# Decays of four turned states made ahead in three buffers, a row's first scan before the last product, and three smaller moves in a state-space kernel

## The reference

```
def _selective_scan(x, x_proj_w, dt_proj_w, dt_proj_b, A_log, Dp):
    A = -jnp.exp(A_log)
    dbc = jnp.einsum('bld,nd->bln', x, x_proj_w)
    delta, Bm, Cm = jnp.split(dbc, [DT_RANK, DT_RANK + D_STATE], axis=-1)
    delta = jax.nn.softplus(jnp.einsum('blr,dr->bld', delta, dt_proj_w) + dt_proj_b)
    deltaA = jnp.exp(delta[..., None] * A)
    BX = delta[..., None] * Bm[:, :, None, :] * x[..., None]
    ...   # hs[t] = deltaA[t] * hs[t-1] + BX[t]
    y = jnp.einsum('blds,bls->bld', hs, Cm)
    return y + Dp * x
...
xn = _layernorm(x, axis=-1)
s = ...   # _selective_scan forward, plus another one backward in time
g = _silu(...)   # xn + 0.3 * (gelu(xn @ w1[e] + b1[e]) @ w2[e] + b2[e]) @ wo + bo
x = x + s * g
```

## Time and profile before

| | before |
|---|---|
| median of 3 runs | 3335.42 us (3330.86 to 3358.07) |
| the profiled execution, its own time | 3326.3 us |
| its span, first to last instruction | 3324.5 us |
| mean granted TensorE clock | 0.92 |
| busy: PE, DVE, ACT, POOL | 76%, 93%, 88%, 91% |
| scans, count and mean | 1024, 2.28 us |
| products on DVE, count and mean | 576, 1.20 us |
| the same on POOL | 448, 2.37 us |
| bx on POOL, count and mean | 608, 2.39 us |

### The profile page before, as it was taken

One profiled execution on the slowest core, in us unless ns is written; L12 is line 12 of the kernel. 1 busy time (PEld: TensorE's weight loads), 2 busy tenths in 40 slices (PEclk: granted clock), 3 DMA queues, 4 the chain that ended last, 5 costly groups with the idle time before them and its releaser, 6 DMA issues. The chain is left out here.

```text
span 3324.5 us, 48313 instructions
## 1 busy us (share of the span) xinstructions
PE 2535.4 (76%) x15766; PEld 2032.0 (61%) x15766; DVE 3085.7 (93%) x2027; ACT 2911.6 (88%) x5434; POOL 3009.6 (91%) x1422
## 2 busy tenths in 40 slices
PE   7777777777777777777777777777777777777776
PEld 5666556666566666566666566665666655666655
DVE  3899999999999999999999999999999999999999
ACT  4889889889889889889898899898898988988986
POOL 2899999999999999999999999999999999999997
PEclk9998999988999988999988999988999899998898
DMA  5443344433344443344433444333444434443332
GB/s 156 138 126 110 103 130 122 129 116 114 101 129 129 128 116 108 115 122 129 123 111 100 132 121 133 115 112 104 127 127 125 114 107 123 122 129 116 111 107 60
DMA packets 273359, 394.12 MB, mean 119 GB/s; under 512 B 45003, under 2 KB 119508, under 8 KB 273108
## 3 DMA queue, kind: packets, MB, share of 16 engines
q1 hardware_dynamic: 273108, 391.03, 40.0%
HBM read 348.98 MB, written 25.18 MB: 113 GB/s over the span
## 5 line engine op out<-in xcount | busy, mean ns | idle before, releaser
L474 POOL TENSOR_TENSOR bx<-dx,b_sb 128x1024 f32<-128x1024 f32 x608 | 1439.9, 2386 | 53.7 <-DVE hs L849 52.8
L849 DVE TENSOR_TENSOR_SCAN hs<-decay,bx 128x1024 f32<-128x1024 f32 x608 | 1384.5, 2282 | 35.1 <-issue 14.1
L1079 PE MATMUL y<-ident,hc 128*128 128x128 f32 x8192 | 1118.9, 287 | 65.0 <-DVE hc L827 37.2
L1079 PEld LDWEIGHTS y<-ident,hc 128*128 128x128 f32 x8192 | 996.0, 149 | 176.7 <-DVE hc L827 91.6
L462 POOL TENSOR_TENSOR hc<-hs,c_sb 128x1024 f32<-128x1024 f32 x448 | 1057.9, 2373 | 8.7 <-DVE hs L849 8.5
L849 DVE TENSOR_TENSOR_SCAN hs<-decay_sb,decay 128x1024 f32<-128x1024 f32 x416 | 938.5, 2275 | 86.4 <-ACT decay_sb L744 76.9
L744 ACT ACTIVATE decay<-delta,rate 128x511 f32<-128x511 f32 (+1 forms) x1216 | 786.6, 684 | 53.7 <-DVE hs L849 53.3
L827 DVE TENSOR_TENSOR hc<-hs,c 128x1024 f32<-128x1024 f32 x576 | 690.7, 1199 | 34.9 <-PE c L1062 30.5
L585 ACT ACTIVATE dxb<-dxT,btok 128x256 f32<-128x256 f32 x1664 | 706.7, 501 | 0.0
L1054 PE MATMUL decay<-ident,dxb 128*128 128x128 f32 x3328 | 459.0, 283 | 261.1 <-DVE hs L849 261.1
L1054 PEld LDWEIGHTS decay<-ident,dxb 128*128 128x128 f32 x3328 | 383.9, 145 | 384.8 <-issue 322.0
(11 more groups left out here) (126 smaller groups left out, 2317.2 us busy)
## 6 DMA issues: line engine op xcount, KB each, us to landing
b_sb<-b_scratch SPq DMA_DIRECT2D x608, 256.0 KB, 3.3
c_sb<-b_scratch SPq DMA_DIRECT2D x448, 256.0 KB, 3.6
xin<-in_L_attn_x_dram SPq DMA_DIRECT2D x32, 512.0 KB, 6.0
w_sb<-in_L_ffn_W_dram SPq DMA_DIRECT2D x32, 512.0 KB, 3.9
w2o_sb<-w2o_scratch SPq DMA_DIRECT2D x32, 512.0 KB
xres<-in_L_attn_x_dram SPq DMA_DIRECT2D x32, 512.0 KB, 5.3
out_dram<-og SPq DMA_DIRECT2D x32, 512.0 KB, 4.4
dbc<-high SPq DMA_DIRECT2D x64, 128.0 KB, 2.3
```

Source lines behind the costliest of these rows:

```text
L474: nc.gpsimd.tensor_tensor(bx[:, i % RING, :, :], dx[:, g, :, :], b_sb[:, i % BRING, :].unsqueeze(1).broadcast_to([P, DT, T]), ALU.mult).th ...
L849: V.tensor_tensor_scan(hs[:, s % HSLOTS, :, :].rearrange("p k t -> p (k t)")[:, u], factor.rearrange("p k t -> p (k t)")[:, u], data.rearr ...
L1079: ins = M(yps[:, c, k * P:(k + 1) * P], hc[:, s % RING, k, c * P:(c + 1) * P], ident[:, :], start=False, stop=(s == ADDED[-1]), is_transpo ...
```

## The change

`TSLOTS` goes from 2 to 3. ScalarE makes the decays of states 22, 24 and 26 at steps 14, 15 and 16 (ahead of that step's drain), and that of 28 at step 23. At step 30 its `copy_dxT` for the next batch row moves behind `make_decay`. VectorE makes the product of state 31 behind the next batch row's first scan. SiLU writes over its input zz, and the buffer `gate` goes away. GpSimd's `residual` moves from step 5 to step 3, and its `shift_of` from step 4 to step 6. The decays of turned states get semaphores of their own, and one more state in each direction gets the one-column instruction.

```diff
-    TSLOTS, XSLOTS = 2, 3
-    MEAN, SCALE, SHIFT, NORM = 0, 1, 4, 6
+    TSLOTS, XSLOTS = 3, 3
+    MEAN, SCALE, SHIFT, NORM = 0, 1, 6, 6
...
-    Y_OUT, Y_RESIDUAL = 1, 5
+    Y_OUT, Y_RESIDUAL = 1, 3
...
-    EDGED = [s for s in range(STEPS) if s in TURNED and TURNED.index(s) - FIRST_TURNED[s // N] < TSLOTS
-             or s in POOL_B and (s % N < DSLOTS or s - DSLOTS in TURNED)]
+    EDGED_SB = [s for s in TURNED if TURNED.index(s) - FIRST_TURNED[s // N] < TSLOTS]
+    EDGED = [s for s in POOL_B if s % N < DSLOTS or s - DSLOTS in TURNED]
+
+    AHEAD = {14: 22, 15: 24, 16: 26, 23: 28}
...
             def silu(row):
                 act.wait_ge(s_zz, row * 2 + 2)
-                wait(act, s_yg, row)
-                A(gate[:, :, :], zz[:, :, :], ACT.Silu).then_inc(s_gate, 1)
+                A(zz[:, :, :], zz[:, :, :], ACT.Silu).then_inc(s_gate, 1)
...
             def make_decay(row, par, s):
-                if n == 0:
-                    act.wait_ge(s_delta, row * 2 + g + 1)
+                act.wait_ge(s_delta, row * 2 + s // N + 1)
...
             def body(row, par, last):
                 for s in range(STEPS):
+                    if s in AHEAD:
+                        make_decay(row, par, AHEAD[s])
                     drain(row, par, s + STEPS)
-                    if not last:
+                    if not last and s != DX_COPY[0]:
                         drain(row + 1, 1 - par, s)
                     if s + DSLOTS < STEPS:
-                        make_decay(row, par, s + DSLOTS)
+                        if s + DSLOTS not in AHEAD.values():
+                            make_decay(row, par, s + DSLOTS)
                     elif not last:
                         make_decay(row + 1, 1 - par, s + DSLOTS - STEPS)
+                    if not last and s == DX_COPY[0]:
+                        drain(row + 1, 1 - par, s)
...
-                V.tensor_tensor(og[:, :, :], yps[:, :, :], gate[:, :, :], ALU.mult).then_inc(s_yg, 1)
+                V.tensor_tensor(og[:, :, :], yps[:, :, :], zz[:, :, :], ALU.mult).then_inc(s_yg, 1)
...
             def body(row, par, last):
                 for s in range(STEPS):
                     scan(row, s)
+                    if s == 0 and row:
+                        times_c(row - 1, STEPS - 1)
                     if s == Y_OUT and not (isinstance(row, int) and row == 0):
                         output(row - 1)
...
-                times_c(row, STEPS - 1)
             rows(body)(dve)
+            times_c(NB - 1, STEPS - 1)
             output(NB - 1)
```

More of the change, by code:

```diff
@@ L169, in mamba_moe_block @@
         w2T = w2T_sb.rearrange("p a (j k f) -> p (a j) k f", k=DT, f=P)
-        w2o_st = (og, gate)
+        w2o_st = (og, zz)
         dps = [pb2("decay0", [P, DT, T]), pb2("decay1", [P, DT, T])]
@@ L595, in absolute @@
                 wait(act, s_dx, (row - 1) * 2 + 1 - g)
-                wait(act, s_decay, (row - 1) * DT * STEPS + (1 - g) * DT * N)
+                wait(act, s_decay, DT * ((row - 1) * NBX + (1 - g) * (N - FIRST_TURNED[1])))
+                wait(act, s_decay_sb, DT * ((row - 1) * NT + (1 - g) * FIRST_TURNED[1]))
                 A(delta[:, g * (1 + par), k, :], bank[:, :], ACT.Relu, bias=dtb[:, g, k:k + 1]).then_inc(s_relu, 1)
@@ L725, in _, with decay_of, cut_of @@
             copy_dxT(0, 1)
+            def decay_of(row, par, s, to, k):
+                g, n = s // N, s % N
+                later = 1 - g
+                cols = slice(0, T) if k != later else slice(1, T) if g == 0 else slice(0, T - 1)
+                return A(to[:, k, cols], delta[:, g * (1 + par), k, cols], ACT.Exp, scale=rate[:, g, k, n:n + 1])
+            def cut_of(s, to):
+                later, edge = (1, 0) if s < N else (0, T - 1)
+                return A(to[:, later, edge:edge + 1], eps[:, :], ACT.Identity, scale=0.0)
             def make_decay(row, par, s):
-                g, n = s // N, s % N
-                if n == 0:
-                    act.wait_ge(s_delta, row * 2 + g + 1)
+                act.wait_ge(s_delta, row * 2 + s // N + 1)
                 if s in TURNED:
@@ L734, in make_decay @@
                     to = decay_sb[:, i % TSLOTS, :, :]
+                    if s in EDGED_SB:
+                        cut_of(s, to).then_inc(s_edge_sb, 1)
+                    for k in range(DT):
+                        decay_of(row, par, s, to, k).then_inc(s_decay_sb, 1)
                 else:
@@ L737, in make_decay @@
                     to = dps[s % DSLOTS]
[L739 to L744, removed]
+                    if s in EDGED:
+                        cut_of(s, to).then_inc(s_edge, 1)
+                    for k in range(DT):
+                        decay_of(row, par, s, to, k).then_inc(s_decay, 1)
             act.wait_ge(s_rate, 1)
@@ L800, in gate_input @@
                 if v == 0:
-                    wait(dve, s_gate, row)
+                    wait(dve, s_yg, row)
                 V.scalar_tensor_tensor(zz[:, 2 * v:2 * v + 2, :], fps[:, :].rearrange("p (c d) -> p c d", c=2), 0.3,
@@ L835, in scan @@
                     dve.wait_ge(s_bxT, i + 1)
+                    if s in EDGED_SB:
+                        dve.wait_ge(s_edge_sb, row * len(EDGED_SB) + EDGED_SB.index(s) + 1)
+                    dve.wait_ge(s_decay_sb, DT * i + DT)
                     data, factor = dps[s % DSLOTS][:, :, :], decay_sb[:, i % TSLOTS, :, :]
@@ L839, in scan @@
                     dve.wait_ge(s_bx, i + 1)
+                    if s in EDGED:
+                        dve.wait_ge(s_edge, row * len(EDGED) + EDGED.index(s) + 1)
+                    dve.wait_ge(s_decay, DT * i + DT)
                     data, factor = bx[:, i % RING, :, :], dps[s % DSLOTS][:, :, :]
-                if s in EDGED:
-                    dve.wait_ge(s_edge, row * len(EDGED) + EDGED.index(s) + 1)
-                dve.wait_ge(s_decay, row * DT * STEPS + DT * s + DT)
                 used = s - HSLOTS
```

2 lines of the change are left out of this document (1 added, 1 removed).

## The result

The changed kernel takes 3226.68 us (median of 4 runs) against 3333.14 us for the kernel before (median of 4): the medians differ by 106 us. The ratio, 0.966 (95% interval 0.961 to 0.971), is that of the fast runs alone, because one run of the changed kernel fell in the chip's slower state (3323.69 us at a granted TensorE clock of 0.80). The forecast was 3248 (3217 to 3290). The profiled execution took 3226.65 us with a span of 3224.9, so 99.6 us less than the profiled one of before.

The account below looks back on a forecast made before the run. VectorE was taken as the bound, standing still about 5 us a row, largely for late ScalarE decays. Terms 2.25 + 0.25 + 0.33 - 0.09 = 2.74 us a row, about 87 us; 3239 plus 9.1 gives 3248 us (3217 to 3290).

Parts of the forecast that it names:

- Decays made ahead: ScalarE, steps 14 to 16: three decays fit in waits for TensorE; VectorE's waits at scans 22 and 24 go, 2.25 us a row.
- 20, 28 and 29: VectorE's smaller waits at these scans shrink or go, 0.25 us a row together.
- the allowance for the median above the profiled execution: 9.1 us added at the end, since the three-run median lay that far above the profiled 3326.3 us.
- The moved product at 0: VectorE, row's start: the C wait moves from state 31's product to ahead of scan 2; gain 0.
- about 1 us earlier: GpSimd, new order: it waits for og instead of rsq and comes about 1 us earlier to everything behind.
- The copy at step 30: ScalarE, row's end: decay 0 fills the wait for turned dx, the second copy starts sooner; 0.33 us a row.
- The added semaphores: Waits for things long done, costed at nothing; would show in "issue", upper bound 0.7 us a row.
- 1 is left: GpSimd, product 27 ahead of scan 31: 2.54 us ahead, loses 2.5 and gains 1, so 1 us left.
- Rival D: Waits at 22 and 24 come back at 23 to 31 because GpSimd cannot follow: 3328 us; chance 0.06.
- A: Row's start: ScalarE's chain begins sooner by the product's C wait, winning 30.5 us more: 3217 us; chance 0.11.
- B: Row's end: TensorE's granted clock sets row length; all long rows 3274 us (chance 0.09), all short 3237.
- C: Steps 14 to 16: decays made ahead do not hide; all late 3375 us (chance 0.04), part 3290 (0.10).

Follow-up runs that it names:

- the last kernel: Changed kernel with state 15's scaling at step 12, decay 26 at step 21, residual sum at step 4, first lg product at step 26: 3208.58 us.
- the kernel ahead of it: Changed kernel with state 15's scaling at step 12 instead of 10, decay 26 at step 21 instead of 16, residual sum at step 4: 3208.66 us.

## Why the prediction was right

**Decays made ahead.** Right in mechanism, place and fit. I had margins of 0.37, 0.38 and 0.22 us between the decays and TensorE's results; the waits left are 1.01, 0.27 and 0.11. (The first is larger because decays 14 and 15 came earlier.) Without the table the gain is nothing, with it alone 72 us. The size was low: I took the listed waits, 2.22 us a row, as the cost. A wait is listed from the end of the instruction before, and that end runs 0.1 us into the next instruction even where nothing waits. By scan starts, the two steps gave 1.19 and 1.28 us, 2.47. For 20, 28 and 29 I had 0.25 where it was 0.53 (0.14, 0.24, 0.15), in part by the same slip. This term was 0.5 us a row, 16 us, too small, and it is the largest part of the 21 us (3248 against 3227) that I was off. Another 9 us are the allowance for the median above the profiled execution, which the changed kernel did not need (its profiled execution and its median are both 3226.7). The two together are more than 21; smaller items, the last row above all, go the other way.

**The moved product at 0.** Right for the kernel before, and right that scan 2 doesn't come sooner by it: from scan 31's start to scan 2's it is 14.33 us on the average, 0.31 less than the 14.64 of before, and that is the copy's part, as the run without the copy shows (14.69). But the 0 is not what it is worth in the changed kernel, where undoing it costs 31 us. My way from scan 31's end to og, 9.6 us, has no C wait in it; so the product's effect was in GpSimd's "about 1 us earlier", which I booked as slack and not as time. The sum came out because it credited the whole gain to the late decays, which could be had in full only with GpSimd in time. Alone they gave 72 of my 87; that the 0 did no harm is luck.

**The copy at step 30** was 0.33 a row in the sum, for an earlier decay 2. Undoing it costs 0.31, because the second copy, decay 2 and scan 2 come later, as I said. I had missed the wait at scan 0 for decay 0; nothing in the trace hangs on it.

**The added semaphores** I had costed at nothing, and said where they would show if they did. Something shows there: scan 1 comes 0.35 us later in every kernel with the third buffer and its semaphores (last section). Whether they are the cause is open.

**GpSimd.** "About 1 us earlier" was right: bx 16 was ready 2.81 us ahead of its scan before and 4.00 in the changed kernel. That "1 is left" at product 27 was too good; 0.33 was, because scan 31 comes sooner by more than I had put, and because the 2.54 us that I started from was one batch row's, where the average was 2.2. Rival D (GpSimd cannot follow) did not come, but it was near, and one step of my argument against it was wrong: "without that gain nothing is left and nothing is lost". With GpSimd's order undone 29 us are lost, with the product moved back 31. My arithmetic against it used GpSimd's work, 93.2 us a row. The quantity that mattered was the loop, 97.6.

**The rivals.** A's time (3217) was nearer to the result than the forecast's, and its mechanism is false: only moving the product changes nothing, and the wait ahead of scan 2 is there. B was seen: the changed kernel's rows run in three lengths from 97.5 to 98.1 us. C did not come; the three decays hide.

## What to carry to other kernels

When one engine is late at a few points, look for its own waits earlier in the same period, and check each piece of work against the end of the wait that is to hide it. With two or three engines near 95%, work out the loops through them (what releases whom until the first is reached again) and not only the work of each: in this kernel an edit outside the longest loop measured as nothing, and the same edit inside it at nearly its full size, so edits that do nothing without the main one were worth a third of the gain with it. Take the cost of a wait from the distances of starts, not from the listed idle time.

## What the runs showed of the hardware

TensorE's granted clock and the row length settle into a pattern. In the last kernel (the lg product at step 26) the second turn of dx ended 2.62 and 1.48 us after scan 31's end, in turn, for the same instructions; the sums ahead of it ran slower in one kind of row. Over nine microseconds around it the granted clock was 0.63 and 0.62 of full speed, so at its low level (1.2 GHz) for some three quarters of the time in both kinds:

```profile
1731.00:1740.00 9.00, 6.87 (x34) 0.63 0.22 75
1829.00:1838.00 9.00, 7.59 (x43) 0.62 0.23 79
```

(Windows of TensorE: length, busy us, granted clock, DMA.) TensorE's first turn of dx took 1.06 us at one of these row ends and 0.60 at the other:

```profile
1738.07 1.06 PE L1004 MATMUL front<-ident,dx 128*128 128x128 f32 x4
...
1835.93 0.60 PE L1004 MATMUL front<-ident,dx 128*128 128x128 f32 x4
```

The granted clock was 0.50 in the first of these and 1.00 in the second. What differs is where in the chain the low clock falls. TensorE's stretch from the product that releases it (1734.07 and 1832.03) to the end of the second turn is the same matmuls without a gap:

```profile
1734.07:1742.14 8.07, 8.07 (x43) 0.62 0.26 90
1832.03:1838.95 6.92, 6.92 (x43) 0.73 0.24 78
```

A shorter row can move that point, and so give back part of what it gained. The last experiment is such a case (0.6 us a row won at 29 and 31, 0.8 lost at scan 2), but the clock is only part of it. Two row ends of the kernel ahead of it (the lg product still at step 25):

```profile
1633.87:1641.13 7.26, 7.26 (x43) 0.69 0.19 44
1730.98:1737.50 6.52, 6.52 (x42) 0.77 0.12 44
```

That stretch starts behind product 29, ahead of scan 31. When scan 31 loses its wait of 0.44 us, the stretch does not start sooner, so its end falls 0.44 us later against scan 31 at any clock. The rest, 0.6 us, is the stretch itself, 7.5 us on the average instead of 6.9, at a lower granted clock. No run here changes the clock alone. The Trainium skill, TensorE: Matmul & The Clock Gate, Part 1, says that the clock is throttled by default and activity releases it. The traces agree in so far as the low clock comes where TensorE has waited: 2.63 and 1.4 to 2.1 us in the six microseconds ahead of these two row ends. I had drawn from it that the idle stretch at the row's start keeps its half clock, and it does (granted 0.50 from 1658.7 to 1662.7 in the changed kernel), and that shorter waits elsewhere could only help. These rows do not bear the second out: it says nothing on where the switch falls.

Left open: in every kernel with the third buffer and the semaphores that come with it, scan 1 starts 0.35 us later behind the statistics (5.50 instead of 5.16 us after scan 0 with the moved product, 4.37 instead of 4.02 without), although its decay is ready 2.8 us and its bx 4.5 us ahead. The trace shows VectorE's own wait instruction for it issued 0.36 us later. No run takes this apart. By the row lengths it could be worth up to 0.35 us x 31 = 11 us, an estimate, and only where the loop binds: scan 2 waits for ScalarE in the changed kernel, whatever scan 1 does.
